# Attention softmax on groups of three tiles, folded key slots, halved value matmuls, three accumulators and new engine orders

## The chip, the cores and the metric

The kernel runs on one core of one Trainium2 chip. The metric is the device time of one execution in microseconds (us). TensorE is PE, VectorE is DVE, ScalarE is ACT, GpSimd is POOL, and SP is the engine that issues nearly all the DMAs here.

## The reference

Input `x` is 8 batches of 1024 tokens with 512 channels. Each row is layer-normalised to `xn`. The result is `x + attention(xn) + ffn(xn)`.

```
qkv = xn @ w_qkv                              # 512 -> 1536
starts = arange(0, 1024 - 4 + 1, 2)           # windows of 4 tokens, one every 2
win = qkv[:, starts[:, None] + arange(4)]
dots = einsum(q, k) per window and head (8 heads of 64) * 512 ** -0.5
o = softmax(dots) @ v ;  y = o @ w_out + b_out
out[idx] += y                                 # overlapping windows are added
ffn(x): q = fp4 quantise-dequantise in blocks of 16
        (silu(q(x) @ q(w_gate).T) * (q(x) @ q(w_up).T)) -> q -> @ q(w_down).T   # 512 -> 1408 -> 512
```

## The kernel before

The kernel has two parts, one after the other, with a barrier between them. `attention` works through the 8 batches and writes its result and the normalised rows to DRAM; `feed_forward` then works through 64 tiles of 128 rows. The change is in `attention` alone.

A batch is 8 tiles of 128 tokens, and one more "edge" tile made of the tokens around the borders of 32-token blocks, whose windows straddle them. The nine tiles are taken in the order 0, 1, 2, 3, edge, 4, 5, 6, 7 (`order`), and a number `a` in the code is a place in that order. For a batch PE does 16 chunks of q and k (`project_qk`, q0 to q15), 8 tiles of v (`project_v`), 9 times scores (`scores`), 9 times the product with v (`attend`), and 8 output projections (`project_out`). Each chunk or projection is 12 float16 matmuls of 512 columns (three products of high and low halves, four contraction pieces). Scores and `attend` are float32.

Each engine has its own program, an order written out by hand: a string of steps, one letter and one number each. `batches` runs two strings. The second string of batch b and the first of batch b+1 make the body of a loop of six turns, and before and behind it stand unrolled copies. A `+` means that the step belongs to the next batch, a `'` to the batch before, and a `*` that the step stands only in the loop. Letters of PE: q, v, s, a, p as above. DVE: t statistics, n normalise, m mask and maxima, u sums, w transposes of weights, g packing of edges, d adding of edges, f finish (adds the projection to the residual), A, R, O the steps of a unit of feed-forward weights (six units are quantised in each loop turn, between the attention steps). ACT: x high half of rows, q and v the copies out of the accumulators, e exponential, o copy of the attended values, h high half of them, B and H its part of a unit. POOL: r root, l low half of rows, b bias, s shift, w weights, o low half of outputs, V and X its part of a unit. SP: l loads of x, k stores of normalised rows, t transposes of rows, e edge values, r and s residual in and out, L, T, S load, transpose and store of a unit, M and Z weights. An engine does its steps strictly in this order, so a step that waits holds up all behind it.

In the softmax, 32 queries of a block meet 32 keys; each query belongs to up to two windows, so the masked scores `sm` exist twice (128 x 2 x 8 heads x 32). Scores land in the PSUM tile `sps`, one tile at a time. `mask_scores` (L635, L640) adds the masks and takes the maxima; POOL's `shift` (L505) subtracts them; ACT's `exponential` (L803); `sums` (L645 to L649); POOL's `weigh` multiplies (L510) and adds both windows (L514); `turn_weights` (L656) transposes by four instructions of 32 partitions into `pt`, whose other blocks stay zero; `attend` (L911) multiplies 128 keys by 128 queries for each head into `ops`; `attended` (L813) copies out. The accumulators `acc0` and `acc1` take q, k and v in turn: chunk n waits until ACT has emptied the one of chunk n-2. `prj` is a single accumulator: `project_out` waits for DVE's `finish` (L680) of the tile before.

Of the kernel before, what the change touches and what calls it, by code (L numbers as in the profile page):

```python
# [15 lines left out]
P = 128  # L16
# [14 lines left out]
ATT = TPB + 1  # L31
EDGE = TPB
# [16 lines left out]
def constants():  # L49

    t = np.arange(P) % BLK
    s = np.arange(BLK)
    pt, ps = t[:, None] // 2, s[None, :] // 2
    first = np.where((ps == pt - 1) | (ps == pt), 0.0, NEG)
    second = np.where((ps == pt) | (ps == pt + 1), 0.0, NEG)
    edge = np.where(t[:, None] // WIN == s[None, :] // WIN, 0.0, NEG)
    masks = np.stack([np.stack([first, second], 1), np.stack([edge, edge], 1)], 1)
    valid = np.ones((P, 2, 2, HEADS))
    valid[:, 0, 0] = (t >= 2)[:, None]
    valid[:, 0, 1] = (t < BLK - 2)[:, None]  # L60
    valid[:, 1, 1] = 0.0
    valid[:WIN, 1, 0] = 0.0
    count = np.full((P, 3), 2.0)
    count[:2, 0] = 1.0
    count[P - 2:, 2] = 1.0
    small = np.concatenate([masks.reshape(P, -1), valid.reshape(P, -1), count], 1).astype(np.float32)
    return small, np.eye(P, dtype=np.float16)
# [5 lines left out]
NSMALL = 2 * 2 * BLK + 2 * 2 * HEADS + 3  # L73
# [128 lines left out]
def attention(nc, x, w_qkv, w_out, b_out, w_gate, w_up, w_down, small, part, normed, ready, late, wsc, raw,  # L202
# [3 lines left out]
    with ExitStack() as ctx:  # L206
# [17 lines left out]
        cst = sb("cst", [P, NSMALL])  # L224
        bias = sb("bias", [P, 3, C])
        sc = sb("sc", [P, 20])
        mask = cst[:, 0:4 * BLK].rearrange("p (v w s) -> p v w s", v=2, w=2)
        valid = cst[:, 4 * BLK:4 * BLK + 4 * HEADS].rearrange("p (v w h) -> p v w h", v=2, w=2)
        count = cst[:, NSMALL - 3:NSMALL]

# [8 lines left out]
        sm = sb("sm", [P, 3, 2, HEADS, BLK])  # L239
        mx = sb("mx", [P, 3, 2, HEADS])  # L240
        rs = sb("rs", [P, 3, 2, HEADS])
        rv = sb("rv", [P, 3, 2, HEADS])
        pw = sb("pw", [P, HEADS, BLK])
        pt = sb("pt", [P, HEADS, P])
# [29 lines left out]
        s_done, masked, maxed, shifted, exped = sem("s_done"), sem("masked"), sem("maxed"), sem("shifted"), sem("exped")  # L274
        summed, inverse, weighed = sem("summed"), sem("inverse"), sem("weighed")
        scaled, p_done, p_turned = sem("scaled"), sem("p_done"), sem("p_turned")
# [3 lines left out]
        pt_zero = sem("pt_zero")  # L280
# [20 lines left out]
        def unit(b, j):  # L301
# [10 lines left out]
                     qkv_done: QKV, qkv_out: QKV, packed: 4, s_done: ATT, masked: ATT,  # L312
                     maxed: ATT, shifted: ATT, exped: ATT, summed: ATT, inverse: ATT, weighed: ATT, scaled: ATT,
                     p_done: ATT, p_turned: ATT, pv_done: ATT, o_out: ATT, o_edge: TPB, o_full: TPB, o_hi: TPB,
# [16 lines left out]
        def _(sp):  # L331
# [110 lines left out]
            def first_edge(b, n):  # L442

                if isinstance(b, int) and b == 0:
# [19 lines left out]
        def _(pool):  # L464
# [38 lines left out]
            def shift(b, a):  # L503
                pool.wait_ge(maxed, at(b, ATT, a))
                pool.tensor_tensor(sm[:, a % 3], sm[:, a % 3], mx[:, a % 3].unsqueeze(3).to_broadcast([P, 2, HEADS, BLK]),  # L505
                                   ALU.subtract).then_inc(shifted, 1)

            def weigh(b, a):
                pool.wait_ge(weighed, at(b, ATT, a))
                pool.tensor_tensor(sm[:, a % 3], sm[:, a % 3], rv[:, a % 3].unsqueeze(3).to_broadcast([P, 2, HEADS, BLK]),  # L510
                                   ALU.mult).then_inc(scaled, 1)
                pool.wait_ge(scaled, at(b, ATT, a))
                pool.wait_ge(p_turned, at(b, ATT, a - 1))
                pool.tensor_tensor(pw[:, :], sm[:, a % 3, 0], sm[:, a % 3, 1], ALU.add).then_inc(p_done, 1)  # L514
# [12 lines left out]
            def value_unit(b, j):  # L527
# [4 lines left out]
                                   ALU.mult).then_inc(f["valued"], 1)  # L532

# [9 lines left out]
            def all_tops(b, n):  # L543

                if isinstance(b, int) and b == 0:
# [691 lines left out]
```

## Time and profile before

| | |
|---|---|
| time, median of 3 runs | 2427.28 us (2427.17 to 2428.37) |
| the profiled execution, its own time | 2427.4 us |
| its span in the trace | 2425.6 us |
| busy: PE, DVE, POOL, ACT | 2219.1, 1778.7, 1291.1, 697.3 us |
| first matmul of the feed-forward part | 1044.5 us |

Busy time is time in which an engine executes something other than register, branch, semaphore and DMA-issuing instructions. A time stamp counts from the start of the span. A matmul's modelled length is longer than the distance between two of a series, so work on PE is better read from one start to the next. The loop body begins, on PE, with the scores of the edge tile (`sps<-qke`): at 141.9, 258.3, 380.5, 502.0, 622.9, 745.6 us, and the unrolled copies behind the loop at 865.4 and 967.9 us.

### The profile page before, as it was taken

Reading aid. Unit: us, or ns where it says so; the run is one execution under the profiler, and the core shown is the slowest. Engines: PE = TensorE matmul, PEld = TensorE weight load, DVE = VectorE, ACT = ScalarE, POOL = GpSimd, SP = SyncE. Lnnn points to the kernel's source line nnn. Section 1 sums busy time; section 2 is a strip of 40 time slices with the busy share of each in tenths; the row PEclk is TensorE's granted clock in tenths of the full one; section 3 lists DMA queues with packets and bytes.
Section 4 is the critical chain, followed back from the end, with each engine's and each line's share of the span. In section 5 each row is a group of like instructions: output and inputs, shape, how many; then the busy total and the mean of one; then the engine's idle time right before and its main releaser. Section 6 shows DMA issues by size and latency. Waiting matters only on the chain.

```text
span 2425.6 us, 44720 instructions
## 1 busy us (share of the span) xinstructions
PE 2219.1 (91%) x15552; PEld 1073.9 (44%) x15552; DVE 1778.7 (73%) x3446; ACT 697.3 (29%) x1055; POOL 1291.1 (53%) x988
## 2 busy tenths in 40 slices
PE   1698888888888999589999999999999999999998
PEld 0344444444444444244444444444444444444443
DVE  5478786878686864657777777877777778777774
ACT  1233333333333332222222222222222222222221
POOL 2166555666555663535555555555555555555553
PEclk9899999999999999699999999999999999999999
DMA  6445454545455552433333333333333333333332
GB/s 222 133 105 140 118 138 118 141 120 137 121 133 123 135 117 82 154 107 76 83 88 87 78 85 88 79 84 83 88 88 80 84 88 79 82 85 87 76 80 62
DMA packets 447389, 251.81 MB, mean 104 GB/s; under 512 B 365250, under 2 KB 371922, under 8 KB 447252
## 3 DMA queue, kind: packets, MB, share of 16 engines
q1 hardware_dynamic: 445860, 244.88, 41.6%
q10 hardware_dynamic: 1104, 4.19, 0.5%
q8 instruction: 90, 1.47, 0.3%
q0 software_dynamic: 288, 0.87, 0.1%
q14 instruction: 47, 0.39, 0.1%
HBM read 98.91 MB, written 59.77 MB: 65 GB/s over the span
## 4 chain that ended last, share of the span: by engine, by line
PE 55%; DVE 1%; DMA 0%; POOL 0%; issue 0%; POOLq 0%; ACT 0%; SPq 0%; DVEq 0%
PE dn L1186 12%; PE gu L1171 6%; PE gu L1172 6%; PE gu L1175 6%; PE gu L1173 6%; PE gu L1176 6%; PE gu L1174 6%; PE dn L1188 6%; DMA ht<-hh 0%; POOL hv L152 0%; DVE hv L188 0%; DVE hv L186 0%; POOLq L940 0%; DVE hv L1067 0%; DVE hs L162 0%
## 5 line engine op out<-in xcount | busy, mean ns | idle before, releaser
L858 PE MATMUL acc<-late 128*128 128x512 f16 x2304 | 530.5, 388 | 98.2 <-DMA late<-xh 59.6
L1186 PE MATMUL dn<-late,ht 128*128 128x512 f16 x1408 | 430.0, 380 | 5.3 <-DMA ht<-hh 5.3
L858 PEld LDWEIGHTS acc<-late 128*128 128x128 f16 x2304 | 224.5, 99 | 387.2 <-issue 85.2
L1067 DVE SCALAR_TENSOR_TENSOR hv<-gu,row_gains,sg 128x512 f32<-128x512 f32 (+1 forms) x192 | 129.0, 672 | 281.7 <-ACT sg L1131 281.7
L152 POOL TENSOR_TENSOR hv<-hv,hs 128x1408 f32<-128x1408 f32 x64 | 165.6, 2588 | 230.1 <-DVE hv L188 230.1
L1171 PE MATMUL gu<-late,turned 128*128 128x512 f16 (+1 forms) x768 | 278.0, 362 | 5.6 <-PEq L206 5.2
L1172 PE MATMUL gu<-late,turned 128*128 128x512 f16 (+1 forms) x768 | 277.9, 362 | 0.0
L1173 PE MATMUL gu<-late,turned 128*128 128x512 f16 (+1 forms) x768 | 277.8, 362 | 0.0
L1174 PE MATMUL gu<-late,turned 128*128 128x512 f16 (+1 forms) x768 | 277.8, 362 | 0.0
L1175 PE MATMUL gu<-late,turned 128*128 128x512 f16 (+1 forms) x768 | 277.8, 362 | 0.0
L1176 PE MATMUL gu<-late,turned 128*128 128x512 f16 (+1 forms) x768 | 277.8, 362 | 0.0
L1188 PE MATMUL dn<-late,ht 128*128 128x512 f16 x704 | 267.6, 380 | 0.0
L858 PE MATMUL prj<-wo,oh 128*128 128x512 f16 x768 | 192.8, 405 | 51.6 <-DVE res L680 48.1
L147 POOL TENSOR_TENSOR hv<-hv,hs 128x1024 f32<-128x1024 f32 (+1 forms) x128 | 177.3, 1385 | 111.4 <-DVE hs L168 111.4
L157 POOL TENSOR_TENSOR hh<-hv,hh 128x1408 f16<-128x1408 f32 x64 | 182.9, 2857 | 98.9 <-ACT hh L198 98.9
L1186 PEld LDWEIGHTS dn<-late,ht 128*128 128x128 f16 x1408 | 137.9, 98 | 169.1 <-issue 6.9
L198 ACT ACTIVATE hh<-hv 128x1408 f16<-128x1408 f32 x64 | 88.1, 1377 | 366.0 <-POOL hv L152 366.0
L1131 ACT ACTIVATE sg<-gu,row_gains 128x512 f32<-128x512 f32 (+1 forms) x192 | 120.0, 642 | 163.9 <-PE gu L1176 163.8
L193 ACT ACTIVATE hm<-hv 128x1024 f32<-128x1024 f32 (+1 forms) x128 | 101.1, 790 | 227.3 <-POOL hv L147 227.3
L510 POOL TENSOR_TENSOR sm<-sm,rv 128x512 f32<-128x512 f32 x72 | 84.4, 1172 | 144.5 <-DVE rv L649 143.8
L635 DVE TENSOR_TENSOR sm<-sps,cst 128x512 f32<-128x512 f32 x72 | 48.0, 666 | 138.6 <-PE sps L897 138.6
L152 POOL TENSOR_TENSOR raw<-raw,scales 128x512 f32<-128x512 f32 x64 | 67.7, 1058 | 144.0 <-DVE raw L188 144.0
(122 smaller groups left out, 3601.9 us busy)
## 6 DMA issues: line engine op xcount, KB each, us to landing
late<-in_L_attn_x SPq DMA_DIRECT2D x64, 256.0 KB, 3.5
normed<-late SPq DMA_DIRECT2D x64, 256.0 KB, 2.2
res<-in_L_attn_x SPq DMA_DIRECT2D x64, 256.0 KB, 2.9
attended<-res SPq DMA_DIRECT2D x64, 256.0 KB, 2.6
raw<-normed SPq DMA_DIRECT2D x64, 256.0 KB, 2.7
pr<-attended SPq DMA_DIRECT2D x64, 256.0 KB, 2.6
out<-fo SPq DMA_DIRECT2D x64, 256.0 KB, 2.1
ready<-turned SPq DMA_DIRECT2D x36, 256.0 KB
```

The costliest lines, as they stand in the source:

```text
L147: pool.tensor_tensor(blocks(v), blocks(v), spread(s[2]), ALU.mult).then_inc(q["scaled"], 1)
L152: pool.tensor_tensor(blocks(v), blocks(v), spread(s[3]), ALU.mult).then_inc(q["valued"], 1)
L157: pool.tensor_tensor(h[:, 1], v, h[:, 0], ALU.subtract).then_inc(q["low"], 1)
L858: last = pe.matmul(out, lhsT, rhs, start=(at == 0), stop=(at == n - 1))
L1171: pe.matmul(g, x_hi, g_hi, start=(c == 0), stop=False)
L1172: pe.matmul(g, x_hi, g_lo, start=False, stop=False)
L1173: pe.matmul(w, x_hi, u_hi, start=(c == 0), stop=False)
L1174: pe.matmul(w, x_hi, u_lo, start=False, stop=False)
L1175: pe.matmul(g, x_lo, g_hi, start=False, stop=(c == KC - 1))
L1176: last = pe.matmul(w, x_lo, u_hi, start=False, stop=(c == KC - 1))
L1186: last = pe.matmul(dps[k][:, :], ht[:, k, at], w_hi, start=(at == 0), stop=(at == 2 * FC - 1))
L1188: pe.matmul(dps[k][:, :], ht[:, k, at], w_lo, start=False, stop=False)
```

## The change

Softmax now works on groups of three tiles (`GT = 3`, three groups in a batch: 0 1 2, 3 edge 4, 5 6 7). The scores of a group are written at once (96 matmuls). DVE adds one mask, which keeps only keys next to the query, to all three tiles (768 columns), and folds the 32 keys to 8 slots by a maximum over the four keys of a slot (L661; only one of the four is not masked). The two windows are then made on 8 slots (`sm` is 128 x 2 x 3 x 8 x 8 = 384 columns). Shift, sums and weighing are DVE's, POOL only spreads the finished weights of each tile back to 64 keys (`spread_weights`), DVE turns them with one transpose over 128 partitions, and `attend` is done by two 64-key halves with 64 queries each, into two PSUM banks. A third accumulator for q, k and v is there, so a chunk waits for the one of three before. The low half of a feed-forward weight unit (`low_unit`) goes from DVE to POOL. All five engines have new order strings. `pt` and `pw` exist twice; `pt` needs no zeros.

```
-        sm = sb("sm", [P, 3, 2, HEADS, BLK])
-        pw = sb("pw", [P, HEADS, BLK])
-        pt = sb("pt", [P, HEADS, P])
+        sa = sb("sa", [P, GT * HEADS, BLK])
+        slots = sb("slots", [P, GT, HEADS, SLOTS])
+        sm = sb("sm", [P, 2, GT, HEADS, SLOTS])
+        pg = sb("pg", [P, GT, HEADS * SLOTS])
+        pw = sb("pw", [P, 2, HEADS, 2, BLK])
+        pt = sb("pt", [P, 2, HEADS, 2 * BLK])
-        acc = [ctx.enter_context(nc.psum_tensor(f"acc{i}", [P, 512], F32)) for i in range(2)]
+        acc = [ctx.enter_context(nc.psum_tensor(f"acc{i}", [P, 512], F32)) for i in range(3)]
-        ops = ctx.enter_context(nc.psum_tensor("ops", [P, KC, P], F32))
+        ops = ctx.enter_context(nc.psum_tensor("ops", [P, 2, 512], F32))
...
-            def shift(b, a):
-                pool.wait_ge(maxed, at(b, ATT, a))
-                pool.tensor_tensor(sm[:, a % 3], sm[:, a % 3], mx[:, a % 3].unsqueeze(3).to_broadcast([P, 2, HEADS, BLK]),
-                                   ALU.subtract).then_inc(shifted, 1)
-
-            def weigh(b, a):
...
+            def spread_weights(b, a):
+
+                pool.wait_ge(p_done, at(b, NG, a // GT))
+                pool.wait_ge(p_turned, at(b, ATT, a - 2))
+                pool.tensor_tensor(pw[:, a % 2].rearrange("p h b (g s) -> p h (b g) s", s=SLOTS),
+                                   pg[:, a % GT].rearrange("p (h s) -> p h s", s=SLOTS).unsqueeze(2)
+                                   .to_broadcast([P, HEADS, 2 * BLK // SLOTS, SLOTS]),
+                                   spread_to.rearrange("p (n s) -> p n s", s=SLOTS).unsqueeze(1)
+                                   .to_broadcast([P, HEADS, 2 * BLK // SLOTS, SLOTS]),
+                                   ALU.mult).then_inc(p_spread, 1)
...
+            def mask_scores(b, g):
+
+                dve.wait_ge(s_done, at(b, NG, g))
+                dve.wait_ge(gathered, at(b, NG, g - 1))
+                dve.tensor_tensor(sa[:, :, :].rearrange("p (i e n) s -> p i e (n s)", i=GT, e=2),
+                                  sps[:, :, 0:GT * P].rearrange("p e (i n) -> p i e n", i=GT),
+                                  near.unsqueeze(1).to_broadcast([P, GT * HEADS, BLK]), ALU.add).then_inc(masked, 1)
+                dve.wait_ge(masked, at(b, NG, g))
+                dve.wait_ge(windowed, at(b, NG * 2, 2 * g - 1))
+                dve.tensor_reduce(slots[:, :, :, :].rearrange("p i h s -> p (i h) s"),
+                                  sa[:, :, :].rearrange("p n (g s) -> p n s g", s=SLOTS),
+                                  AX.X, ALU.max).then_inc(gathered, 1)
+
+            def window_scores(b, g):
+
+                dve.wait_ge(gathered, at(b, NG, g))
+                dve.wait_ge(p_done, at(b, NG, g - 1))
+                for w in range(2):
+                    dve.tensor_tensor(sm[:, w], slots[:, :, :, :],
+                                      windows[:, g % 2, w].unsqueeze(2).to_broadcast([P, GT, HEADS, SLOTS]),
+                                      ALU.add).then_inc(windowed, 1)
+
+            def shift_scores(b, g):
+
+                dve.wait_ge(windowed, at(b, NG * 2, 2 * g + 1))
+                dve.tensor_reduce(mx[:, :], flat, AX.X, ALU.max).then_inc(maxed, 1)
+                dve.wait_ge(maxed, at(b, NG, g))
+                dve.tensor_tensor(flat, flat, mx[:, :].unsqueeze(2).to_broadcast([P, 2 * GT * HEADS, SLOTS]),
+                                  ALU.subtract).then_inc(shifted, 1)
...
+            def weigh(b, g):
+
+                dve.wait_ge(weighed, at(b, NG, g))
+                dve.tensor_tensor(flat, flat, rs[:, :].unsqueeze(2).to_broadcast([P, 2 * GT * HEADS, SLOTS]),
+                                  ALU.mult).then_inc(scaled, 1)
+                dve.wait_ge(scaled, at(b, NG, g))
+                dve.wait_ge(p_spread, at(b, ATT, GT * g - 1))
+                dve.tensor_tensor(pg[:, :, :].rearrange("p i n -> p (i n)"),
...
             def turn_weights(b, a):
-                dve.wait_ge(p_done, at(b, ATT, a))
-                dve.wait_ge(pv_done, at(b, ATT, a - 1))
-                for j in range(P // BLK):
-                    r = slice(j * BLK, (j + 1) * BLK)
-                    last = dve.transpose(pt[r, :, r], pw[r])
-                last.then_inc(p_turned, 1)
+                dve.wait_ge(p_spread, at(b, ATT, a))
+                dve.wait_ge(pv_done, at(b, ATT, a - 2))
+                dve.transpose(pt[:, a % 2].rearrange("p h q -> p (h q)"),
+                              pw[:, a % 2].rearrange("p h b s -> p (h b s)")).then_inc(p_turned, 1)
...
-                pe.wait_ge(qkv_out, at(b, QKV, q_use(n) - 2))
+                pe.wait_ge(qkv_out, at(b, QKV, q_use(n) - 3))
...
                 for h in range(HEADS):
-                    last = pe.matmul(ops[DH * (h % 2):DH * (h % 2) + DH, h // 2, :],
-                                     vals[:, h * DH:(h + 1) * DH], pt[:, h % 2 * (HEADS // 2) + h // 2, :],
-                                     start=True, stop=True)
+                    for g in range(2):
+                        r = slice(2 * BLK * g, 2 * BLK * (g + 1))
+                        last = pe.matmul(ops[DH * (h % 2):DH * (h % 2) + DH, g, h // 2 * DH:(h // 2 + 1) * DH],
+                                         vals[r, h * DH:(h + 1) * DH], pt[r, a % 2, h % 2 * (HEADS // 2) + h // 2, :],
+                                         start=True, stop=True)
                 last.then_inc(pv_done, 1)
```

PE's strings, as an example of the new orders:

```
-                    "s0 a7' p4' q8 q9 q10 s1 a8' p5' q11 q12 q13 s2 a0 p6' q14 q15 v4 "
-                    "s3 a1 p7' v5 v6 v7",
-                    "s4 a2 W1+ q0+ q1+ q2+ s5 a3 q3+ q4+ q5+ s6 a4 q6+ q7+ v0+ s7 a5 v1+ p0 v2+ "
-                    "s8 a6 p1 v3+ p2 p3 W2+ ",
+                    "p6' v4 s1 a0 v5 a1 p7'",
+                    "v6 s2 W1+ v7 a2 q0+ q1+ q2+ a3 q3+ q4+ q5+ a4 q6+ q7+ v0+ p0 a5 v1+ s0+ p1 a6 v2+ p2 a7 v3+ q8+ "
+                    "q9+ q10+ q11+ p3 q12+ q13+ p4 a8 q14+ p5 W2+ q15+",
```

On PE, in the loop body of before, behind the first three q chunks, scores and values of neighbouring tiles stand between every three chunks (here the sixth tile's scores and the fourth tile's values):

```order
L897 MATMUL sps<-qk 32x32 x32
L908 REGISTER_ALU
L911 MATMUL ops<-pt,v 64x128 x8
L866 REGISTER_ALU
L858 MATMUL acc1<-late 128x512 x12
L866 REGISTER_ALU
L858 MATMUL acc0<-late 128x512 x12
L866 REGISTER_ALU
L858 MATMUL acc1<-late 128x512 x12
```

On PE, at the same chunks of the changed kernel, no scores stand here, a value step has 16 small matmuls, and three accumulators take turns:

```order
L961 MATMUL ops<-pt,v 64x64 x16
L911 ISA
L912 ISA
L904 MATMUL acc0<-late 128x512 x12
L912 REGISTER_ALU
L904 MATMUL acc1<-late 128x512 x12
L904 MATMUL acc2<-late 128x512 x12
L951 REGISTER_ALU
L955 REGISTER_ALU
L961 MATMUL ops<-pt,v 64x64 x16
```

The scores have moved to three places in the body, 96 matmuls each.

On DVE, late in the loop body of before, one tile's softmax (mask, maxima, sums of the tile before it, and the four transposes) lies around a finish and a weight unit's low half:

```order
L632 REGISTER_ALU
L635 TENSOR_TENSOR sm<-sps,cst 128x512
L640 TENSOR_REDUCE mx<-sm 128x16
L656 STREAM_TRANSPOSE pt<-pw 32x8x32 x4
L678 REGISTER_ALU
L680 SCALAR_TENSOR_TENSOR res<-prj,sc,res 128x512
L714 TENSOR_TENSOR split<-raw,split 128x512
L645 TENSOR_REDUCE rs<-sm 128x16
L647 RECIPROCAL rs<-rs 128x16
L649 TENSOR_TENSOR rv<-rs,cst 128x16
```

On DVE, near the end of the changed loop body, one group of three tiles goes through nearly whole:

```order
L656 TENSOR_TENSOR sa<-sps,cst 128x768
L661 TENSOR_REDUCE slots<-sa 128x192
L670 TENSOR_TENSOR sm<-slots,cst 128x192 x2
L676 REGISTER_ALU
L677 TENSOR_REDUCE mx<-sm 128x48
L679 TENSOR_TENSOR sm<-sm,mx 128x384
L703 REGISTER_ALU
L705 STREAM_TRANSPOSE pt<-pw 128x512
L685 TENSOR_REDUCE rs<-sm 128x48
L687 RECIPROCAL rs<-rs 128x48
L689 TENSOR_TENSOR rs<-rs,cst 128x48
L694 TENSOR_TENSOR sm<-sm,rs 128x384
```

What was POOL's (shift and weighing) now stands in DVE's own row of steps, once for three tiles; the low half of the unit is gone from DVE.

## Rows read from the trace of the kernel before

**Rows 1.** The page's first part: busy time, share, instructions of each engine.

```profile
PE 2219.1 (91%) x15552; PEld 1073.9 (44%) x15552; DVE 1778.7 (73%) x3446; ACT 697.3 (29%) x1055; POOL 1291.1 (53%) x988
```

**Rows 2.** Stretches: length, busy PE, PEld, DVE, ACT, POOL, PE clock, DMA share, GB/s.

```profile
49.20:141.90 92.70, 72.98 (x580) 33.45 (x580) 51.12 (x88) 23.74 (x38) 26.08 (x30) 0.87 0.52 148
141.90:258.30 116.40, 103.89 (x1105) 50.71 (x1105) 95.22 (x181) 40.77 (x71) 73.26 (x69) 0.97 0.54 127
258.30:865.40 607.10, 528.04 (x5520) 259.36 (x5520) 468.35 (x905) 200.01 (x349) 365.19 (x345) 0.95 0.52 129
865.40:967.90 102.50, 99.84 (x1105) 50.25 (x1104) 54.28 (x121) 32.60 (x54) 50.60 (x50) 1.00 0.32 87
967.90:1044.50 76.60, 42.38 (x530) 22.15 (x530) 44.99 (x95) 15.38 (x25) 38.72 (x36) 0.75 0.52 173
1044.50:2425.60 1381.10, 1371.94 (x6720) 657.97 (x6720) 1039.44 (x2026) 375.34 (x509) 726.16 (x442) 1.00 0.36 81
```

**Rows 3.** PE in order of time: start, length, work, idle time before it.

```profile
955.73 0.76 PE L897 MATMUL sps<-qk 64*32 64x32 f32 x64
956.41 1.09 PE L911 MATMUL ops<-pt,v 128*64 128x128 f32 x16
957.44 2.76 PE L858 MATMUL prj<-wo,oh 128*128 128x512 f16 x12
960.04 7.93 PE L858 MATMUL acc<-late 128*128 128x512 f16 x36
```

**Rows 4.** Waits in five loop turns (258.3 to 865.4 us), total, times, longest.

```profile
ACT split L829 <- DMA turned<-split: 128.9, 20, 11.3
PE acc L858 <- ACT qk L792: 30.9, 22, 2.5
PE prj L858 <- DVE res L680: 28.3, 14, 3.4
```

**Rows 5.** PE in order of time at one turn of the loop.

```profile
622.93 0.27 PE L897 MATMUL sps<-qke 64*32 64x32 f32 x9 [0.83 <-issue]
626.57 0.81 PE L897 MATMUL sps<-qke 64*32 64x32 f32 x55 [3.37 <-issue]
```

**Rows 6.** Instruction groups of those five turns: busy us, mean ns, idle before.

```profile
L656 DVE STREAM_TRANSPOSE pt<-pw 32x256 f32<-32x256 f32 x180 | 78.1, 434 | 4.0 <-PE ops L911 2.1
L510 POOL TENSOR_TENSOR sm<-sm,rv 128x512 f32<-128x512 f32 x45 | 54.0, 1200 | 92.3 <-DVE rv L649 91.7
L505 POOL TENSOR_TENSOR sm<-sm,mx 128x512 f32<-128x512 f32 x45 | 47.1, 1047 | 62.7 <-DVE mx L640 62.7
L514 POOL TENSOR_TENSOR pw<-sm 128x256 f32<-128x256 f32 x45 | 42.4, 943 | 3.9 <-POOL sm L510 0.8
L640 DVE TENSOR_REDUCE mx<-sm 128x16 f32<-128x512 f32 x45 | 30.9, 686 | 1.5
L645 DVE TENSOR_REDUCE rs<-sm 128x16 f32<-128x512 f32 x45 | 30.6, 681 | 34.5 <-ACT sm L803 34.3
L635 DVE TENSOR_TENSOR sm<-sps,cst 128x512 f32<-128x512 f32 x45 | 29.6, 658 | 66.3 <-PE sps L897 66.3
L714 DVE TENSOR_TENSOR split<-raw,split 128x512 f16<-128x512 f32 x30 | 24.4, 814 | 8.0 <-ACT split L829 7.3
L897 PE MATMUL sps<-qke 64*32 64x32 f32 x320 | 5.2, 229 | 20.1 <-issue 20.1
```

**Rows 7.** PE in order of time, before the loop: the two long waits.

```profile
92.26 0.88 PE L897 MATMUL sps<-qk 64*32 64x32 f32 x64 [9.27 <-DMA ve<-oe]
103.59 10.59 PE L858 MATMUL acc<-late 128*128 128x512 f16 x36 [10.44 <-DMA late<-xh]
```

**Rows 8.** PE in order of time, the end of the attention part.

```profile
1036.56 2.75 PE L858 MATMUL prj<-wo,oh 128*128 128x512 f16 x12 [0.94 <-DVE res L680]
1044.48 0.58 PE L1171 MATMUL gu<-late,turned 128*128 128x512 f16 x1 [5.17 <-PEq L206]
```

**Rows 9.** One DVE line, 240 to 968 us: durations ns minimum, median, maximum.

```profile
L714 DVE TENSOR_TENSOR split<-raw,split x30: 691/693/1385, 288.7 to 846.4; 128x512 f16<-128x512 f32 x30
```

More of the change, by code:

```diff
@@ L31 @@
 ATT = TPB + 1
+GT = 3
+NG = ATT // GT
+SLOTS = 8
 EDGE = TPB
@@ L53, in constants, with slots @@
     pt, ps = t[:, None] // 2, s[None, :] // 2
[L54 to L62, printed above, removed]
+    near = np.abs(ps - pt) <= 1
+    first = (ps == pt - 1) | (ps == pt)
+    second = (ps == pt) | (ps == pt + 1)
+    edge = t[:, None] // WIN == s[None, :] // WIN
+    def slots(keys):
+        return keys.reshape(P, BLK // SLOTS, SLOTS).any(1)
+    inner = np.stack([slots(first), slots(second)], 1)
+    outer = np.stack([slots(edge), slots(edge)], 1)
+    valid_in = np.ones((P, 2, HEADS))
+    valid_in[:, 0] = (t >= 2)[:, None]
+    valid_in[:, 1] = (t < BLK - 2)[:, None]
+    valid_out = np.ones((P, 2, HEADS))
+    valid_out[:, 1] = 0.0
+    valid_out[:WIN, 0] = 0.0
+    kinds = [[0, 0, 0], [0, 1, 0]]
+    windows = np.stack([np.stack([(inner, outer)[k] for k in g], 2) for g in kinds], 1)
+    valid = np.stack([np.stack([(valid_in, valid_out)[k] for k in g], 2) for g in kinds], 1)
+    own = np.arange(P)[:, None] // BLK % 2 == np.arange(2)[None, :]
+    spread = own[:, :, None] & near[:, None, :]
     count = np.full((P, 3), 2.0)
@@ L65, in constants @@
     count[P - 2:, 2] = 1.0
-    small = np.concatenate([masks.reshape(P, -1), valid.reshape(P, -1), count], 1).astype(np.float32)
+    masks = [np.where(near, 0.0, NEG), np.where(windows, 0.0, NEG), valid, np.where(spread, 1.0, 0.0), count]
+    small = np.concatenate([m.reshape(P, -1) for m in masks], 1).astype(np.float32)
     return small, np.eye(P, dtype=np.float16)
@@ L72 @@
 UNITS = 3 * FC
-NSMALL = 2 * 2 * BLK + 2 * 2 * HEADS + 3
+SMALL = [BLK, 2 * 2 * GT * SLOTS, 2 * 2 * GT * HEADS, 2 * BLK, 3]
+SMALL_AT = [sum(SMALL[:n]) for n in range(len(SMALL) + 1)]
 def hold(engine, passed):
@@ L223, in attention @@
         wo = sb("wo", [P, 2, KC, C], F16)
-        cst = sb("cst", [P, NSMALL])
+        cst = sb("cst", [P, SMALL_AT[-1]])
         bias = sb("bias", [P, 3, C])
         sc = sb("sc", [P, 20])
-        mask = cst[:, 0:4 * BLK].rearrange("p (v w s) -> p v w s", v=2, w=2)
-        valid = cst[:, 4 * BLK:4 * BLK + 4 * HEADS].rearrange("p (v w h) -> p v w h", v=2, w=2)
-        count = cst[:, NSMALL - 3:NSMALL]
+        near, windows, valid, spread_to, count = [cst[:, SMALL_AT[n]:SMALL_AT[n + 1]] for n in range(5)]
+        windows = windows.rearrange("p (v w i s) -> p v w i s", v=2, w=2, i=GT)
+        valid = valid.rearrange("p (v n) -> p v n", v=2)
         mv = sb("mv", [P, TPB, 2])
@@ L532, in value_unit, with low_unit @@
                                    ALU.mult).then_inc(f["valued"], 1)
+            def low_unit(b, j):
+                pool.wait_ge(f["high"], at(b, PER, j))
+                pool.tensor_tensor(wh[:, 1], raw[:, j % 3, :], wh[:, 0], ALU.subtract).then_inc(f["low"], 1)
             def first_scale(b, k):
@@ L710, in round_unit @@
                 dve.scalar_tensor_tensor(v, wm, ROUND_MIN, v, ALU.max, ALU.subtract).then_inc(f["rounded"], 1)
-            def low_unit(b, j):
-                dve.wait_ge(f["high"], at(b, PER, j))
-                dve.tensor_tensor(wh[:, 1], raw[:, j % 3, :], wh[:, 0], ALU.subtract).then_inc(f["low"], 1)
             def first_scales(b, k):
@@ L789, in qk_out @@
                 act.wait_ge(qkv_done, at(b, QKV, q_use(n)))
[L790 removed]
+                act.wait_ge(s_done, at(b, NG, turn[4 * g + 3] // GT - NG))
                 act.wait_ge(packed, at(b, 4, 2 * g + 1 - 4))
[L792 removed]
+                act.activation(qk[:, c, g * 512:(g + 1) * 512], acc[q_use(n) % 3][:, :], ACT.Copy,
                                scale=QKV_GAIN).then_inc(qkv_out, 1)
@@ L872, in project_v, with scores @@
             def project_v(b, i):
-                pe.wait_ge(qkv_out, at(b, QKV, v_use(i) - 2))
+                pe.wait_ge(qkv_out, at(b, QKV, v_use(i) - 3))
                 tok = slice(i * P, (i + 1) * P)
-                three_products(acc[i % 2][:, :], [((xt[:, 0, k, tok], xt[:, 1, k, tok]),
+                three_products(acc[v_use(i) % 3][:, :], [((xt[:, 0, k, tok], xt[:, 1, k, tok]),
                                                    (wq[:, 0, k, 2 * C:], wq[:, 1, k, 2 * C:]))
                                                   for k in range(KC)]).then_inc(qkv_done, 1)
-            def scores(b, a):
-                tile = order[a]
-                if tile == EDGE:
+            def scores(b, g):
+                tiles = order[GT * g:GT * g + GT]
+                pe.wait_ge(qkv_out, at(b, QKV, max(q_use(8 * (n // 4) + 7) for n in tiles if n != EDGE)))
+                if EDGE in tiles:
```

116 lines of the change are left out of this document (51 added, 65 removed), and 23 rows, old and new, of tables (dst, scale, u, v).

## The prediction

> **What bounds the kernel now.** I read first the page's busy shares [rows 1]: PE is at 91%, DVE at 73%. A mean over two parts says little, so the stretches come next [rows 2]. The feed-forward part (1381.1 us) has PE busy for 1371.9 of them; the change does not touch it, and it stays as it is. All that can change lies in the first 1044.5 us: a start (to 141.9 us), a first turn of the loop (116.4), five more (607.1, so 121.4 each), the unrolled batch behind it (102.5), and an end (76.6).
>
> Then PE in order of time, for the price of its work [rows 3]. From one start to the next, a tile's scores take 0.68 us (956.41 - 955.73), a tile's values 1.03, a chunk or projection 2.60. A batch has 32 chunks and projections: 83.2, 9 x 0.68 = 6.1, 9 x 1.03 = 9.3, together 98.6 us. The unrolled batch takes 102.5, so it runs nearly at PE's own pace. It has no weight units; DVE is busy for 54.3 of its 102.5 us. A loop turn has six of them, DVE busy 93.7, POOL 73.0 (a fifth of [rows 2]), and takes 121.4: 22.8 us more than PE's work. PE's busy time is 528.0 / 5 = 105.6, that is 7.0 above 98.6, at a granted clock of 0.95 where the unrolled batch has 1.00 [rows 2]. The remaining 15.8 is idle, and the waits name it [rows 4, 5, 6]: 6.2 a turn for ACT's copy out of an accumulator, 5.7 for DVE's finish (`prj` is single), and 4.0 (20.1 / 5) where the loop jumps back and PE waits for nothing shown, 0.83 and 3.37 us on both sides of nine matmuls. No engine is full. In-order queues meet late: ACT, for one, stands 128.9 / 5 = 25.8 us a turn before the high half of a unit, for a transpose of the unit before, and the copies that PE wants stand behind it. So time is in the order of steps, and in how often one tile's softmax crosses between engines: PE, DVE, POOL, ACT, DVE, POOL, DVE, PE, nine times a batch.
>
> **The change, part by part (per batch).**
>
> DVE, removed: mask 29.6, maxima 30.9, sums 30.6, transposes 78.1, together 169.2 / 5 = 33.8, and the low half of units 24.4 / 5 = 4.9 [rows 6]; the small reciprocals stay alike and are left out. Added, per group: 768 + 768 columns, then 2 x 192, 2 x 384, 384, 384, 192. That is 3648 columns. No row has these sizes. By proportion to 0.67 us for 512 [rows 6] it is 4.8; if each smaller operation cost as much as 512 columns, seven of them (4.7) and the two of 768 (2.0), it is 6.7. A transpose of 128 x 512 has twice the columns of the 0.434 us one and four times its partitions: 0.43 to 0.87 each, 1.3 to 2.6 a group. Sum 6.1 to 9.3, times three 18 to 28. DVE goes from 93.7 to between 73 and 83; I take 76, nearer the proportion, since these rows are long streams.
>
> POOL, removed: (54.0 + 47.1 + 42.4) / 5 = 28.7. Added: nine spreads of 512 columns at 1.20, the price of the like-shaped multiply, 10.8, and six low halves at the same 1.2, 7.2. From 73.0 to 62.3; were the broadcast spread to cost double, 73, still below PE.
>
> ACT: nine exponentials become three of 384 columns; ACT was busy 40.0 and is no bound.
>
> PE: the same scores, in groups. Values: 32 instructions of 64 columns for 16 of 128 per tile. The nearest row from below is the scores' 64 in 0.68 us, 10.6 ns each: 0.34 us a tile. From above, no gain: 1.03. I take 0.65, the middle, as both halves sit in different rows of the array. PE's floor becomes 83.2 + 6.1 + 5.9 = 95.2 (92.4 to 98.6). The Trainium skill, TensorEngine Tiling (Array Packing), Instruction Overhead, says each matmul costs about 60 cycles, so that a small dimension should not be cut; as an estimate at 2.4 GHz, 32 x 25 ns = 0.8 us a tile, which would make the floor 96.5. The scores' 10.6 ns each, on eight small tiles, do not agree with it as a spacing.
>
> The orders. I set PE's new string on paper at 2.60 a chunk and asked for each step of the other engines whether it is ready. Between the scores of group 1 and q0, which needs the accumulator of v5, PE has a0 v5 a1 p7 v6 s2 v7 a2, 14 us. ACT empties v5 only behind the exponential of that group, which needs DVE's mask, fold, windows, maxima and shift, about 4 us, plus what stands ahead of them. From scores to the group's first values it is 7 chunks and s2 (some 21 us) for group 1, about 41 for group 2 and 50 for group 0, where the softmax chain is about 9 us. The projections are now mostly apart by another chunk, so the 0.94 us behind each finish [rows 8] is covered. A unit's high half on ACT comes a few steps behind the transpose it waits for; the tightest (unit 3) has about 1 us. DVE's first step in a turn, a unit's scales, waits for its load, which SP issues behind three moved row stores, edge values and residuals: about 4 us late by my paper, covered since q0 to q5 stand before the values that DVE's next steps feed. DMA share 0.54 [rows 2] of 116 us is 63 us a batch, 0.62 of a turn of 101. So I cost SP's moves at nothing; if that cover were gone it would be those 4 us. The third accumulator gives a late copy 2.6 us more. Of the 6.2 and 5.7 of waits I leave 1 in all. The jump now meets 12 slow matmuls first, then a group's scores; I leave 2.5 of its 4.0. With fewer stops the clock should return to nearly that of the unrolled batch; I leave 2 of 7.0. A turn: 95.2 + 1 + 2.5 + 2 = 100.7, say 101.
>
> The start: PE waited 9.3 us for the edge zeros' DMA, behind the weights of `w_out`, and 10.4 for the transposes of tiles 4 to 7 [rows 7]. Both steps now stand elsewhere: the first scores ahead of that wait, and the row loads and transposes ahead of it on SP. So 19.7 less, and 5.2 less as v6 and v7 now lie in the loop's turn: 141.9 - 24.9 = 117; I take 119, as two weight maxima still stand between on DVE.
>
> The end: it holds those two v tiles (5.2), scores of a group (2.1), then the edge tile's values and its passage to the first projection, ready at about 17. Eight projections with the 0.94 gap [rows 8] are 8 x 2.60 + 7 x 0.94 = 27.4, some 3 us more for a8 and the first feed-forward rows on POOL, and 5.2 to the barrier [rows 8]: 52.6, say 53 against 76.6.
>
> Sum: 119 + 98.5 (first turn, no jump) + 5 x 101 + 97.5 (unrolled: 95.2 + 2.3) + 53 = 873, against 1044.5. With 1381.1, the span is 2254. The profiled execution took 2427.4 by its time and 2425.6 by its span, 1.8 more; its time is that of the median (2427.28) within 0.1. So 2256 us.
>
> **The rivals.**
>
> *The lock (0.21).* DVE's shift, weighing and addition now read two SBUF operands, and POOL reads too. The low half of a unit took 691, 693 and at most 1385 ns [rows 9]: exactly double when something stood in its way. If each of the six such operations of a group loses up to 1.2 us (one POOL step), DVE gains 22 us, near 98 of work; then DVE leads and a turn comes to about 111. That is 6 x 10 more: 2316. Against it: the mean of L714 is 0.81 [rows 6], only 0.12 above its median, and POOL is busy less. The Trainium skill, SBUF — State Buffer, Who interferes with whom, says that a DVE instruction with two SBUF inputs contends with POOL's reads and that one blocks fully; by that rule, the longest of rows 9 agrees.
>
> *The waits only move (0.12).* The order might not be what pays: if a turn stays at 118, as DMA (63 us) and six units' trips through five engines set it, only the start, the unrolled batch and the end gain: 2256 + 6 x 17 = 2358. For it: the ACT wait of 25.8 a turn. Against: no queue's sum comes near 118.
>
> *Slower: the bursts starve (0.05).* At the jump PE got nine matmuls and waited 3.37 us for the next 55 [rows 5]. If every further 55 of a group's 192 (96 in two passes) had to wait so, it would be 3.5 x 3.37 = 11.8 us a group, 35 a turn: 95.2 + 35 + 4 = 134. Seven such batches before the end, some 34 above mine, and 12 at the end: 2256 + 250 = 2506. It turns slower from 25 us a turn, 8 a group, on. Against it: in the straight run 64 behind slow matmuls went without a wait [rows 3]. The Trainium skill, Runtime: NRT & Kernel Launch, Instruction fetch mechanics, says that crossing a block of instructions is mostly hidden and a taken branch is not; rows 3 and 5 agree.
>
> **How the numbers follow.** Forecast 0.60 (a turn from 97 to 105, 2228 to 2285), lock 0.21, moved waits 0.12, starving 0.05, and 0.02 below the forecast. The range runs from the PE floor's low bound (92.4: 2256 - 8 x 2.8 = 2234, a little less for a shorter end) to the lock's time with some more on DVE, 2325. Of the moved waits, 0.02 might end within 0.2%, which is what a measurement of this kernel can tell from no change (about 5 us). So faster 0.93, same 0.02, slower 0.05.
>
> **What would show it.** In the new profile: a loop turn on PE of 97 to 105 us; 32 value instructions a tile from 0.34 to 1.03 us; DVE busy 73 to 83 a turn and POOL about 62; hardly a wait of PE on ACT's accumulator copies; the waits of 9.3 and 10.4 in the start gone and the first turn at about 119; the feed-forward's first matmul near 873. It is wrong if DVE's operations on two operands are stretched, if PE waits for transposed weights (`pt`), if the copy of v5 comes late at q0, or if issue waits stand inside the score groups.

## The result and the profile after

The changed kernel takes 2278.41 us (median of 4 runs, 2275.91 to 2280.72); the kernel before took 2427.23 us in the same measurement. The ratio is 0.9388, with a 95% interval from 0.9371 to 0.9404: 149 us less. The prediction was 2256 us, with a range from 2226 to 2325.

The page of the changed kernel begins with its span and the busy times:

```profile
span 2274.1 us, 46572 instructions
PE 2160.4 (95%) x16704; PEld 1041.8 (46%) x16704; DVE 1638.1 (72%) x3097; ACT 655.9 (29%) x1007; POOL 1220.4 (54%) x880
```

DVE's share is 72% where it was 73% in [rows 1]; its sum is 141 us lower, but so is the span. As before, the stretches say more. The columns are those of [rows 2]; the edges are the starts of PE's loop body, here the v chunk v6:

```profile
50.15:122.80 72.65, 65.49 (x712) 31.00 (x712) 44.18 (x68) 19.56 (x32) 14.43 (x17) 0.98 0.61 167
122.80:221.60 98.80, 96.87 (x1256) 47.61 (x1248) 79.96 (x139) 36.17 (x66) 66.29 (x58) 1.00 0.61 154
221.60:739.30 517.70, 491.78 (x6241) 239.37 (x6241) 364.88 (x680) 174.53 (x320) 327.95 (x286) 0.97 0.59 150
739.30:836.30 97.00, 96.93 (x1249) 48.16 (x1248) 44.46 (x82) 28.10 (x50) 41.03 (x36) 1.00 0.37 99
836.30:893.20 56.90, 37.51 (x537) 17.68 (x536) 36.95 (x68) 12.87 (x22) 31.24 (x26) 0.88 0.76 243
893.20:2274.10 1380.90, 1371.79 (x6720) 657.97 (x6720) 1039.54 (x2026) 375.37 (x509) 726.89 (x442) 1.00 0.36 81
```

Against [rows 2]: the five later turns take 517.7 us instead of 607.1 (103.5 each, not 121.4), the unrolled batch 97.0 instead of 102.5, the end 56.9 instead of 76.6, and the feed-forward part is the same (1380.9). In the unrolled batch PE is busy for 96.93 of 97.00 us: PE's own work is all that is left there.

Where the time went, stretch by stretch, from [rows 2] minus the rows above: start 19.1 us, first turn 17.6, five turns 89.4, unrolled batch 5.5, end 19.7, feed-forward 0.2. Together they are the 151.5 us between the two spans.

PE's waits from 110 to 840 us (total, times, longest), where [rows 4] had 30.9 and 28.3 us in five turns for ACT's copies and DVE's finishes:

```profile
PE acc L904 <- issue: 22.5, 10, 3.2
PE sps L944 <- issue: 3.5, 7, 0.9
PE prj L904 <- DVE res L729: 0.8, 2, 0.5
PE acc L904 <- ACT v L844: 0.8, 1, 0.8
PE acc L904 <- DMA late<-xh: 0.3, 1, 0.3
```

In this stretch hardly anything holds up PE but "issue" (time in which it waited for nothing that the profile shows): the other three sum to 1.9 us. The issue waits are 26.0 us, and 22.5 of them lie at the jump of the loop, as in [rows 5]. PE in order of time around one jump (start, length, work, idle time before):

```profile
421.61 0.44 PE L944 MATMUL sps<-qk 64*32 64x32 f32 x6
422.94 0.68 PE L944 MATMUL sps<-qk 64*32 64x32 f32 x56 [0.90 <-issue]
423.68 0.69 PE L961 MATMUL ops<-pt,v 64*64 64x64 f32 x32
424.31 2.76 PE L904 MATMUL acc<-late 128*128 128x512 f16 x12
427.00 0.69 PE L961 MATMUL ops<-pt,v 64*64 64x64 f32 x32
427.63 2.76 PE L904 MATMUL prj<-wo,oh 128*128 128x512 f16 x12
432.02 0.60 PE L904 MATMUL acc<-late 128*128 128x512 f16 x2 [1.63 <-issue]
435.25 4.02 PE L904 MATMUL acc<-late 128*128 128x512 f16 x10 [2.63 <-issue]
439.20 2.15 PE L944 MATMUL sps<-qk 64*32 64x32 f32 x192
441.28 2.76 PE L904 MATMUL acc<-late 128*128 128x512 f16 x12
```

The projection should end at about 430.2. From there to the scores at 439.2 one chunk of 12 matmuls takes 9.0 us instead of 2.6: two waits (4.3), and matmuls at a low clock behind them (ten in 4.0 us; the granted clock from 435.25 to 439.20 is 0.57, where the ones before the jump have 1.00). That is 6.4 us, and 103.5 - 97.0 is 6.5. A tile's values take 0.63 us (423.68 to 424.31) where they took 1.03 in [rows 3]. One short wait, 0.90, lies inside the score group itself.

The groups of DVE and POOL in the five turns (columns as in [rows 6]):

```profile
L528 POOL TENSOR_TENSOR pw<-pg,cst 128x512 f32<-128x512 f32 x46 | 59.7, 1307 | 0.0
L705 DVE STREAM_TRANSPOSE pt<-pw 128x512 f32<-128x512 f32 x45 | 31.1, 698 | 46.0 <-POOL pw L528 46.0
L661 DVE TENSOR_REDUCE slots<-sa 128x192 f32<-128x768 f32 x15 | 22.7, 1515 | 1.0
L656 DVE TENSOR_TENSOR sa<-sps,cst 128x768 f32<-128x768 f32 x15 | 14.4, 958 | 5.2 <-PE sps L944 5.2
L679 DVE TENSOR_TENSOR sm<-sm,mx 128x384 f32<-128x384 f32 x15 | 12.6, 842 | 0.5
L694 DVE TENSOR_TENSOR sm<-sm,rs 128x384 f32<-128x384 f32 x15 | 8.4, 558 | 0.5
```

DVE now waits 46.0 us for POOL's spread weights in these turns, and no wait of PE for `pt` stands in the list above: it costs PE nothing.

### The profile page after: what moved, and what is told of

The parts are those of the page before. It is cut to its first block, busy times and chain, and to the rows that moved or that the text cites. A ratio compares the mean times of both kernels' runs of the same rounds, so it can differ in the third digit from the quotient of the medians.

```text
span 2274.1 us, 46572 instructions
## 1 busy us (share of the span) xinstructions
PE 2160.4 (95%) x16704; PEld 1041.8 (46%) x16704; DVE 1638.1 (72%) x3097; ACT 655.9 (29%) x1007; POOL 1220.4 (54%) x880
## 4 chain that ended last, share of the span: by engine, by line
PE 59%; DVE 1%; POOL 0%; DMA 0%; issue 0%; POOLq 0%; ACT 0%; SPq 0%; DVEq 0%
PE dn L1235 13%; PE gu L1220 7%; PE gu L1224 7%; PE gu L1225 7%; PE gu L1222 7%; PE gu L1221 7%; PE gu L1223 7%; PE dn L1237 6%; POOL hv L169 0%; DMA ht<-hh 0%; DVE hv L205 0%; DVE hv L203 0%; POOLq L989 0%; DVE hv L1116 0%; DVE hs L179 0%
## 5 line engine op out<-in xcount | busy, mean ns | idle before, releaser
L904 PE MATMUL prj<-wo,oh 128*128 128x512 f16 x768 | 179.5, 384 | 10.5 <-DVE res L729 7.5
L520 POOL TENSOR_TENSOR res<-res,bias 128x512 f32<-128x512 f32 x64 | 85.0, 1329 | 95.7 <-DMA res<-in_L_attn_x 95.6
L837 ACT ACTIVATE qk<-acc 128x512 f32<-128x512 f32 x128 | 75.4, 594 | 178.7 <-PE acc L904 176.7
```

Source lines behind the costliest of these rows:

```text
L904: last = pe.matmul(out, lhsT, rhs, start=(at == 0), stop=(at == n - 1))
```

## The experiments

Each compares with runs of the kernel before on the same chip (2425.7 to 2429.0 us in the three groups). The differences between experiments are read from their medians; the changed kernel is 2278.41. It was not run again in these groups, which ran on other chips; taken from the ratios instead, each difference stated here comes out within 2 us of the same.

**Written-out turns (e1).** Does the jump cost what it seems to?

```
-    with engine.Fori(0, LOOP) as b:
+    for b in range(LOOP):
         follow(second, do, b, True)
         follow(first, do, b + 1, True)
```

> The changed kernel with the six loop turns of attention written out, so that no engine jumps back. Theory: PE sets the pace, and what a turn takes over the unrolled batch (103.5 against 97.0 us) is the jump: 5.1 us of issue waits and a lowered clock behind them. Then five times 6.5 us go: about 2246 us. Rival: the 6.5 us are work of the weight units on other engines that PE waits for, and the wait only changes its name: 2270 to 2280 us.

Measured: 2296.23 us, ratio 0.9461 (0.9444 to 0.9477). Neither: it is slower by 18 us. PE's waits in the whole execution, and two of them in order of time:

```profile
PE sps L944 <- issue: 34.0, 15, 3.3
```

```profile
585.14 0.55 PE L944 MATMUL sps<-qk 64*32 64x32 f32 x35 [3.34 <-issue]
638.55 0.47 PE L944 MATMUL sps<-qk 64*32 64x32 f32 x30 [2.01 <-issue]
```

The jump's waits before slow chunks are gone, and 15 others have come, all inside score groups, two in each batch. A group is 192 matmuls and 192 weight loads in 2 us. My theory of the jump was incomplete: the bursts of the changed kernel wait for instructions too. That is the mechanism of the rival to which I gave 0.05. The burst alone is not the whole condition, though. Of a batch's three groups s2 never waited. In the other two, from 167 us on, the place of the wait moves by one matmul from batch to batch: behind it 39, 38, 37, 36, 35, 34 and 33 matmuls of the group are left in s0, and 34, 33, 32, 31, 30, 29 and 28 in s1. So the waits also hang on the place in PE's instruction stream; what sets that place no run shows.

**The low half back on DVE (e2).** `low_unit` again in DVE's functions, in its order (O4', O5', O0 to O3) near the places where POOL had it, and out of POOL's.

> The changed kernel with the low half of the weight units back on DVE. DVE is busy 72.4 us of a turn of 103.5 and gets some 4.9 more, POOL 7.4 less. Theory (PE sets the pace, DVE has room): no change, 2273 to 2286 us. Rival (DVE's queue is what the old kernel was waiting for, so that its load is what pays): each turn 3 to 5 us longer, 2296 to 2310 us.

Measured: 2277.28 us, ratio 0.9377 (0.9359 to 0.9395). No change, as the first theory has it: in the new orders this part of the change is worth nothing.

**Two accumulators (e3).**

```
-                pe.wait_ge(qkv_out, at(b, QKV, q_use(n) - 3))
+                pe.wait_ge(qkv_out, at(b, QKV, q_use(n) - 2))
...
-                three_products(acc[q_use(n) % 3][:, :], ...
+                three_products(acc[q_use(n) % 2][:, :], ...
```

> The changed kernel with two accumulators for q, k and v instead of three, all else the same. Theory A (the third accumulator only hides late copies of ACT, and the new order puts other ACT steps between the copies): 2 to 6 us more a batch, 2295 to 2325 us. Theory B (the new order alone would do): 2276 to 2284 us. Theory C (the third accumulator is most of the gain): over 2370 us.

Measured: 2295.74 us, ratio 0.9453 (0.9437 to 0.9468). Theory A at its lower end: the third accumulator is worth 17 us in the new order. PE's wait for ACT's q and k copies is back, small (110 to 840 us; the profiled execution is the slowest of the four, 2301.22):

```profile
PE acc L904 <- ACT qk L837: 12.9, 7, 3.2
```

The issue waits are longer too, 29.2 and 4.6 us where they were 22.5 and 3.5, so not all of the 17 us is ACT's copies.

**Values twice (e4).**

```
-                for h in range(HEADS):
+                for h in [*range(HEADS), *range(HEADS)]:
                     for g in range(2):
```

> The changed kernel with each tile's 16 value matmuls done twice. Theory (PE sets the pace everywhere): 9 x 0.63 us more a batch, 8 batches, 45 us: about 2323 us. Rival (PE has hidden room in a batch): half of it or less, under 2300 us.

Measured: 2324.04 us, ratio 0.9575 (0.9544 to 0.9605). 45.6 us more, where 8 x 9 x 0.63 = 45.4 was to come. The interval is 7 us to either side, so the match to a fraction of a microsecond is luck: the issue waits from 110 to 840 us rose by 5 (26.0 to 31.3), while at four of the five jumps the chunk behind now ran at the high clock. Within that, PE sets the pace: a microsecond of its work is about a microsecond of time, and the rival (half or less) is out.

**Scores tile by tile, with the loop (e5).** PE issues the scores of a group in three steps with a slow chunk between; DVE still gets all three at once.

```
-                    "p6' v4 s1 a0 v5 a1 p7'",
-                    "v6 s2 W1+ v7 a2 q0+ q1+ q2+ ... p0 a5 v1+ s0+ p1 a6 v2+ p2 a7 ...
+                    "s3 p6' v4 s4 a0 v5 s5 a1 p7'",
+                    "v6 s6 W1+ v7 s7 a2 q0+ s8 q1+ q2+ ... p0 a5 v1+ s0+ p1 s1+ a6 v2+ s2+ p2 a7 ...
```

> The changed kernel with its loop, but the scores of a group issued one tile at a time, with a chunk or projection of slow matmuls between two tiles on PE; DVE still takes three tiles at once. Theory (PE's small float32 instructions are used up faster than they are supplied when 384 of them come in one burst of 2 us): the 0.4 to 0.9 us waits inside the edge group go, the jump's waits stay: 2268 to 2276 us. Rival (supply is a matter of the jump alone): no change, 2275 to 2282 us, or a little more as DVE gets its scores 3 us later.

Measured: 2329.19 us, ratio 0.9599 (0.9577 to 0.9621), 51 us slower, which neither expected. PE in order of time, the two waits of one turn:

```profile
284.43 4.10 PE L904 MATMUL prj<-wo,oh 128*128 128x512 f16 x12 [3.65 <-DVE res L729]
341.14 4.75 PE L904 MATMUL acc<-late 128*128 128x512 f16 x12 [5.79 <-issue]
```

The waits inside the groups are gone, but the group of the next batch is now complete 5.8 us later (one projection, one chunk and one value step more). On DVE its mask step stands ahead of the finish of p1, and p2 waits for that. The wait of 3.65 us pulls the clock down as well: 12 matmuls in 4.1 to 5.3 us, not 2.76. I had named the delay ("DVE gets its scores 3 us later") and not asked what is queued behind that step. The second line is the jump's wait, also somewhat longer than in the changed kernel.

**The same, written out (e6).**

> The same, and the six loop turns written out. Written out alone gave 2296 us, with 15 issue waits of 1.5 to 3.3 us, all inside groups of scores. Theory (bursts starve): spaced scores leave no such wait, and with no jump a batch takes about 97 us: 2240 to 2250 us. Rival (the supply of instructions to PE is short in the mean over a written-out batch): the waits come back at other places, over 2280 us.

Measured: 2284.51 us, ratio 0.9417 (0.9399 to 0.9434). The issue waits inside the batches are gone (one of 2.1 us is left in the end part), as the theory of the bursts wants. The time misses the theory's range and lies in the rival's (over 2280), but the rival's issue waits are not there: seven waits of 3.5 to 3.7 us for DVE's finish, those of e5, are, with a lowered clock behind six of them, some 36 us in all.

**The next batch's scores one place earlier, written out (e9) and with the loop (e10).** Only the part of PE's string that differs from e5 and e6 is shown.

```
-  v0+ p0 a5 v1+ s0+ p1 s1+ a6 v2+ s2+ p2 a7
+  v0+ p0 s0+ a5 v1+ s1+ p1 s2+ a6 v2+ p2 a7
```

> Written-out turns and scores tile by tile as before this, but the next batch's first three tiles of scores stand one projection earlier on PE (s0 behind p0, s1 behind v1, s2 behind p1), so that DVE has them when its mask step comes. In the last kernel that mask step stood ahead of a finish and cost PE one wait of 3.6 us and some 2.5 us of lowered clock in each of 7 batches, 43 us. Theory: that wait goes and nothing takes its place: 2238 to 2250 us. Rival (PE's slack there is gone, the wait moves to another step): over 2265 us.

Measured: 2248.64 us, ratio 0.927 (0.9255 to 0.9286). It beats both kernels, by 30 and by 179 us. PE's waits in the whole execution:

```profile
PE acc L904 <- DMA late<-xh: 52.6, 3, 49.6
PE prj L904 <- DVE res L729: 8.5, 14, 2.6
PE ops L965 <- DVE pt L705: 4.1, 1, 4.1
PE sps L947 <- issue: 2.4, 1, 2.4
```

and two starts of the edge tile's scores, one batch apart:

```profile
402.17 0.76 PE L947 MATMUL sps<-qke 64*32 64x32 f32 x64
498.92 0.76 PE L947 MATMUL sps<-qke 64*32 64x32 f32 x64
```

A batch takes 96.8 us, as the unrolled batch of the changed kernel (97.0), and no wait in it is longer than 0.2 us.

> The same PE order with the loop. Theory (the jump costs a wait for instructions of 5 to 6 us and some 2.5 us of lowered clock, in five turns): 35 to 45 us above the written-out form: 2275 to 2290 us. Rival (the jump is covered once the scores are spaced): within 15 us of it.

Measured: 2287.19 us, ratio 0.9431 (0.9415 to 0.9446), 39 us above the written-out form: the first theory. One jump, in order of time:

```profile
328.63 5.03 PE L904 MATMUL acc<-late 128*128 128x512 f16 x12 [5.11 <-issue]
```

5.1 us of waiting and 12 matmuls in 5.03 instead of 2.76: 7.4 us, five times 37. With the loop, spacing the scores is a loss of 9 us against the changed kernel; without it, a gain of 48 over e1. One jump in the five, at 538.92, is named as a wait for ACT's v copy (4.65 us) and not as issue. The gain of 48 holds two edits, the spacing (e6 has it alone, 12 us below e1) and the earlier place. Each removal alone loses time, e1 18 us and e10 9; together they gain 30.

**On the kernel before: narrow values (e7), three accumulators (e8), written out (e11).** e7 does the value matmuls in two halves of 64 keys and 64 queries, from the old `pt`; e8 makes the third accumulator, as the change does (`% 3` and the waits); e11 is the edit of e1.

> The kernel before with only the value matmuls changed: two halves of 64 keys and 64 queries, the same weights. PE's work falls by 0.40 us a tile, 3.6 a batch. Theory (the old loop turn is set by queues meeting late, not by PE's sum): less than half of 29 us comes through, 2415 to 2427 us. Rival (PE's work counts in full): 2398 us.

Measured: 2410.22 us, ratio 0.9927 (0.9908 to 0.9947): 15.5 us less, about half of the 29 that left PE and between the two expectations. It is no clean price of the narrow values, because the jump changed with the edit. PE's waits from 258 to 840 us:

```profile
PE acc L859 <- ACT qk L792: 38.1, 21, 4.6
PE prj L859 <- DVE res L680: 33.2, 15, 3.8
PE acc L859 <- DMA late<-xh: 7.6, 3, 2.6
PE sps L898 <- issue: 2.9, 5, 0.7
```

In the kernel before they are 30.0, 28.3, none and 20.1 in the same stretch. So some 16 us of issue waits went as well, and 21 us came back as waits for ACT, DVE and DMA. PE's work was not the pace there, and less so than the half suggests. Why the jump is cheaper in e7 no run shows.

> The kernel before with only a third accumulator for q, k and v. Waits of PE on ACT's copies were 6.2 us a turn. Theory (they show that ACT is late, because of the queues; a third buffer takes part of it): 2400 to 2420 us. Rival A (the two accumulators were the main fault): 2350 to 2385 us. Rival B (the wait goes to the next buffer): 2424 to 2430 us.

Measured: 2419.92 us, ratio 0.998 (0.9967 to 0.9993): 5.8 us less (2 to 8 by the interval), the theory at its upper end. In its five turns the wait for ACT's q and k copies fell from 30.0 to 7.0 us (both from 258 to 840 us), and these stood there:

```profile
PE prj L858 <- DVE res L680: 35.5, 18, 2.8
PE ops L911 <- DVE pt L656: 7.1, 4, 1.8
```

The wait for the finish had been 28.3 [rows 4], that for the turned weights not there. The time moved to the next queue.

> The kernel before with its six loop turns written out. Theory (its score bursts are 128 instructions behind slow matmuls and found their instructions in the straight run; the jump's 4.0 us and the clock behind it go): 20 to 30 us less, 2398 to 2408 us. Rival (other waits take the time, as PE is not the pace there): over 2418 us.

Measured: 2390.9 us, ratio 0.9856 (0.9839 to 0.9872), 37 us less, more than either theory. Of PE's issue waits two are left before the feed-forward part, of 0.95 and 1.05 us, both in the end. Its scores come 128 instructions at a time.

**DVE's fold and transposes twice (e12).** The second fold and the second transpose wait for the first by the same semaphore, whose counts are doubled.

> The changed kernel with DVE's fold of the keys and its transpose of the weights each done twice: 3 x 1.51 + 9 x 0.70 us and 12 small waits, about 12 us a batch more on DVE, 84 of 103.5 us in a turn. Theory (DVE's relief counts only as slack; the chain s to a has more than 10 us of it): 2275 to 2305 us. Rival (the relief of DVE is what the gain came from): 8 x 12 us come back, about 2370 us.

Measured: 2288.76 us, ratio 0.9432 (0.9416 to 0.9448). DVE is busy 419.5 / 5 = 83.9 us a turn instead of 73.0, and the kernel is 10 us slower, not 90. PE's waits on DVE in the whole execution, where the changed kernel has 7.5 and 0.9:

```profile
PE prj L911 <- DVE res L736: 10.5, 10, 2.2
PE ops L968 <- DVE pt L712: 8.2, 4, 5.4
```

This puts back 10.9 of the 20.7 us a turn by which DVE's load fell (93.7 to 73.0).

## Why the prediction was right, and where it was off

**The mechanism** was as forecast: the old turn was set by queues that met late, and in the new orders PE hardly waits for them (1.9 us from 110 to 840 us). e4 shows that PE's work counts in full now, and e7, at half or less, that it did not before. e2 (4.9 us a turn back on DVE) and e12 (10.9) show that up to there DVE's smaller load counts as slack; the whole of the old load was not put back.

**The sum, term by term.** Predicted and measured: start 119 and 122.8; first turn 98.5 and 98.8; five turns 505 and 517.7; unrolled batch 97.5 and 97.0; end 53 and 56.9; feed-forward 1381.1 and 1380.9. The differences are 3.8, 0.3, 12.7, -0.5, 3.9 and -0.2, together 20.0: the 2254.1 of the prediction and the 2274.1 of the span.

**The mis-sized term is the jump.** My turn was 95.2 of work, 1 of waits on engines, 2.5 of the jump's waiting and 2 of clock. A fifth of the row 221.60:739.30 has PE busy for 98.4, which is 3.2 above 95.2 where I left 2, and idle for 5.2, of which 5.1 are issue waits (25.4 in five turns) where I left 2.5; the waits on engines, left at 1, are nearly nothing. I had argued that slow matmuls would cover the jump. The slow chunk right behind it does not cover the wait; it is what waits.

The price was also read too low. I took 4.0 for the old jump, its idle time alone. PE before and behind the jump of [rows 5]:

```profile
614.17 7.93 PE L858 MATMUL acc<-late 128*128 128x512 f16 x36
627.35 1.98 PE L911 MATMUL ops<-pt,v 128*64 128x128 f32 x16
629.26 8.91 PE L858 MATMUL acc<-late 128*128 128x512 f16 x36
638.10 0.76 PE L897 MATMUL sps<-qk 64*32 64x32 f32 x64
```

From 614.17 to 638.10 are 23.9 us for six chunks, one scores step and one values step, which take 17.3 at the prices of [rows 3]. So this jump cost 6.6 with the clock behind it (granted 0.50 in the values step), and the five by the same count 6.1 to 6.7. The changed kernel's costs 6.5 (103.5 against 97.0): the change left the jump as dear as it was. The five old ones sum to 32 of the 37 us that e11 gained; where the other 5 come from was not looked into.

**The start** had the scores' wait for the edge zeros gone, but the wait for the rows' transposes shrank from 10.4 only to 5.6 (91.3 us), which I had taken as gone. **The end** had a wait of 3.0 us for POOL before the first projection and one of 2.6 for DVE before the sixth, both of which then ran at the low clock (12 matmuls in 4.5 and 4.3 us), and 6.9 us to the barrier instead of 5.2.

**Sizes of parts.** PE's values: 0.65 us a tile taken, 0.63 measured. The estimate of 0.8 us from the 60 cycles of the Trainium skill (TensorEngine Tiling (Array Packing), Instruction Overhead) is above it: 32 matmuls in 0.63 us are 20 ns each. DVE: 73.0 a turn, the lower end of 73 to 83 (76 taken). Within it the fold took 1.51 us where proportion gave 1.03; the operations of 192 and 384 columns took 0.36 to 0.56 us undisturbed, between proportion and the price of 512 columns. POOL: 65.6 instead of 62.3; its spread took 1.31, not 1.20.

**The rivals.** *The lock* is there, and small. The shift (L679) took 557 ns at the least and 842 in the mean of the five turns. From 243 to 845 us it started 13 times while an operation of POOL was running, and took 0.71 to 1.65 us; the six times that POOL was idle or began later, it took 0.56. The like-sized multiply (L694) never met POOL in the five turns and took 557 to 559 ns; the two times that it did later, at 768.12 and 851.72, it took 1.43 us. In the five turns the shift lost 4.3 us so, and the window step (L670, 586 ns in the mean and 355 in the median) about 7. It costs PE nothing there, since DVE has slack. My prediction had named stretched DVE operations and issue waits inside the score groups as signs of being wrong; both came, at a size that does not matter to the time. *The waits only move*: seen on the kernel before (e8), not on the changed one. *The bursts starve*: there as waits for instructions inside the bursts. In the changed kernel they are 0.2 to 0.9 us each, 3.5 us in all from 110 to 840 us; in e1 34 us. Spaced scores (e6, e9) have none inside the batches. I had held against it a straight run of 128-instruction groups, three times smaller than the new ones.

**What stays open.** Of the 149 us, the narrow values are worth 29 in the new order by e4's rate (8 x 9 x 0.40, an estimate) and the third accumulator 17. The other 100 or so belong to grouping the softmax and to the new orders together, and 39 us of the whole gain lie in the start and the end; these were not tried apart, since either alone needs an order of its own. Why five turns with a jump got their bursts almost free of waits while the written-out ones did not was not shown either; in the changed kernel the wait inside a burst stands at the same matmul of s1 in every turn (56 left in the group; one more, of 0.17 us, elsewhere), while in e1 its place moves on.

## What to carry to other kernels

When no engine is full and every one waits, write the order of the busiest engine down at its own pace and ask of each step on the other queues when it can be ready: here that gave each stretch within 4 us, but for the jump. Group the steps that cross engines so that each chain has many microseconds of slack; then the other engines' load hardly matters (10.9 us more on DVE in each turn cost 10 in the whole kernel), and what is left is the busiest engine's instruction count, its supply and its clock. Space bursts of small matmuls between slow ones, and check what is queued behind any step that this delays.

## What the runs showed of the hardware

A jump of the PE program cost 3.7 to 4.4 us of waiting in the kernel before, 4.0 to 5.5 in the changed one, 4.7 to 6.5 in e5 and e10, but under 1.5 in e7; outside e7 1.5 to 2.5 us more of lowered clock came with it. Bursts of 384 small PE instructions in about 2 us waited 0.9 to 3.3 us for "issue" in a written-out program (e1); bursts of 128 between slow matmuls did not, inside the batches (e6, e9). The Trainium skill (Runtime: NRT & Kernel Launch, Instruction fetch mechanics) has a taken branch to a far target as a stall for fetching instructions, which agrees with the waits at the jump, and the crossing of a block of instructions as mostly hidden. Whether e1's waits are such crossings no run shows.

Behind PE's waits of 3.65, 5.11 and 5.79 us (e5, e10) the next 12 matmuls took 4.10, 5.03 and 4.75 us instead of 2.76, at a granted clock of 0.66, 0.54 and 0.57 of 2.4 GHz, so mostly at the 1.2 GHz level: there a wait cost 1.3 to 2.3 us more than its length. Not each one did: behind the wait of 3.55 us at 686.05 in e6 they took 2.75.

A DVE maximum over four values that lie 32 bytes apart took 1.51 us for 768 inputs, 2.0 ns each, where the maxima over 32 neighbours took 1.3 ns each [rows 6].
